# A selective scan on one core: two state products per GpSimd instruction, six fixed buffers for scanned states

## The chip, the cores and the metric

The kernel runs on one core of one Trainium2 chip. Its time is the device time of one execution in microseconds (us). Three executions took 8322.33, 8327.16 and 8331.08 us, so the median is 8327.16. The engines are TensorE (PE in the profile, its weight loads PEld), VectorE (DVE), ScalarE (ACT), GpSimd (POOL) and SyncE (SP), whose queue issues all DMAs. PE's clock has two levels, 1.2 and 2.4 GHz; the profile gives the granted clock as a share of the upper one.

## The reference, cut to what matters

The input is 1024 channels of 64 x 64 pixels. A first layer normalises and mixes along channels; its output, as 4096 tokens of 1024, goes through a bidirectional selective scan, which takes most of the time:

```python
def _direction(x_bdl, conv_w, conv_b, xproj_w, dtproj_w, dtproj_b, A_log, Dv):
    xc = conv(x_bdl) + conv_b                      # 4 taps, each of 2048 channels alone
    x_dbl = xc @ xproj_w.T                         # 64 for dt, 16 for B, 16 for C
    dt = x_dbl[..., :64] @ dtproj_w.T + dtproj_b
    Bm, Cm = x_dbl[..., 64:80], x_dbl[..., 80:]
    xc = jnp.clip(xc, -10.0, 10.0)                 # u
    delta = softplus(clip(dt, 1e-05, 1.0) + dtproj_b)
    # for each channel d and each of 16 states n, along the tokens:
    #   h = exp(delta * A[d, n]) * h + (delta * u) * B[n];  y = sum_n h * C[n]
    return y + xc * Dv

y = (y_fwd + y_bwd) * silu(z)
out = y @ out_proj_w.T
```

## The kernel before, in words

The stages run one after another: channel norm, pixel variance, a scan over channels, token norm, `stage_scan`, `stage_out`. The change is all in `stage_scan`, from about 700 to 7280 us.

In `stage_scan` the work is cut into 256 units, `b` in the code: first 128 of the backward direction, then 128 of the forward one. 16 units, one for each block of 128 channels, share a chunk of 512 tokens. A unit has 16 steps, one for each state `n`, and each engine has its own hand-written order within them (its function `unit`); semaphores tie the engines together. While unit b is scanned, the engines also prepare what comes later: delta of unit b + 1 (ACT), the input projection for x 17 units ahead or for z of this unit (PE, L836, copied by ACT at step 7, L1014), the convolution and projection of unit b + 17 (PE L843 and L848). The last 16 backward units have no input projection, the last 16 forward units no convolution.

For each state, ACT writes the decay exp(delta A) into one of two banks `da` (L1074), DVE scans (L1231), and ACT saves the last column (L1054, at the step two later). The scanned state is then multiplied by C and summed over the states in PSUM (`yT`) by transposing matmuls on PE. There are three ways for that:

- 10 states (`VN`) are scanned into PSUM (`h`, two slots), multiplied by DVE (L1241, which also waits for the save of that state) into one of six slots of `hc`, and transposed by PE (L962).
- 4 states (`PN` = 2, 5, 8, 11) are scanned into SBUF (`hs`), multiplied by GpSimd (`weigh_c`, L1188) into `hp`, and transposed by PE (L923) at steps `POOL_AT` = 5, 8, 11, 14.
- 2 states (`TN` = 4, 10) are scanned into `hs`, transposed by PE into `in_ps` at steps 8 and 12 (`turn`, L858), copied by ACT at steps 12 and 15 (L1040), and multiplied with the diagonals of C by PE (`add_turned`, L867). GpSimd makes the diagonals once a chunk (L1154).

`hs` has four slots which the six states of a unit use in turn, so the scan of a state waits until the one four places back has been read. GpSimd also clips xc to u (L1163), forms du = delta u (L1166), and multiplies du with B for four states at a time (`weigh_b`, L1179) into the ring `w` of four groups. Its order in unit b is: weights of group 2; product 2; weights of group 3; product 5; u and du of unit b + 1; product 8; in the first unit of a chunk two diagonals; weights 0 of unit b + 1; product 11; weights 1 of unit b + 1. At step 10 ACT multiplies u with D (`ud`, L1106), which PE adds at step 11 (L954). ACT copies the finished `yT` of unit b - 1 at step 2 of unit b (L1033), once PE has added its last product. SyncE loads xc after du, and at the end of a chunk the B and C rows of the next one (`broadcast`), each group when its last reader in the old chunk is done.

## Time and profile before

| | |
|---|---|
| median of three runs | 8327.16 us |
| profiled execution | 8327.64 us |
| its span, first to last instruction | 8325.9 us |
| busy PE / DVE / ACT / POOL, share of the span | 87% / 87% / 64% / 81% |
| mean granted clock of PE | 0.948 |
| weights with B on POOL, 128x2048 | 1023 of 4541 ns |
| scans on DVE, 128x512 | 2560 of 1280 ns into PSUM, 1536 of 1265 ns into SBUF |
| products with C on DVE / on POOL | 2560 of 678 ns / 1024 of 1276 ns |

How to read it: busy times are of one profiled execution. They are averages over stages, and in the scan stage DVE and POOL are both busy nearly all the time, so what sets the pace has to be read from the waits and from the timeline of a unit. In the timeline neighbours of one kind are merged (x2), and a bracket gives the idle time before a group and what ended it.

### The profile page before, as it was taken

The page shows a single profiled execution, that of the slowest core. Times are in us where ns is not written, and L with a number is a line of the kernel's source. Part 1 is how long each engine was busy: PE and PEld are TensorE (multiplying, and loading weights), DVE is VectorE, ACT ScalarE, POOL GpSimd, SP SyncE. Part 2 cuts the span into 40 slices and gives each one's busy share as a digit, 9 for nine tenths or more (in the row PEclk, how much of TensorE's full clock was granted, in tenths as well). Part 3 has the DMA queues.
Part 4 walks back from the last instruction along what each step waited for, and adds up shares of the span by engine and source line. Part 5 has one row for each costly group of instructions (what it writes and reads, how often), then busy time and mean ns, then how long its engine had stood idle before and what let it go on. Part 6 is the DMA issues. An engine that isn't in the chain of part 4 may idle for free. (4 is left out here: it accounts for less than half of the span.)

```text
span 8325.9 us, 116063 instructions
## 1 busy us (share of the span) xinstructions
PE 7232.1 (87%) x32656; PEld 4473.8 (54%) x32656; DVE 7202.0 (87%) x7790; ACT 5330.5 (64%) x12487; POOL 6737.9 (81%) x2833
## 2 busy tenths in 40 slices
PE   7568989998999899977899899899888987779999
PEld 3243555555555555555555555555555555534444
DVE  6921999999999999999999999999999999934444
ACT  3743777777777777776777777777777776610000
POOL 0612999999999999999999999999999999921110
PEclk9789999999999999988899999999999998889999
DMA  3273232313232323221323232323232322154342
GB/s 86 76 199 135 66 117 69 117 66 117 69 117 66 117 69 117 67 98 43 105 76 127 80 129 75 128 80 127 76 128 81 124 98 82 44 199 139 134 141 75
DMA packets 540822, 843.96 MB, mean 101 GB/s; under 512 B 112576, under 2 KB 260032, under 8 KB 522816
## 3 DMA queue, kind: packets, MB, share of 16 engines
q1 hardware_dynamic: 540224, 837.03, 30.5%
q8 instruction: 248, 4.06, 0.2%
q14 instruction: 350, 2.87, 0.1%
HBM read 583.83 MB, written 253.02 MB: 101 GB/s over the span
## 5 line engine op out<-in xcount | busy, mean ns | idle before, releaser
L1179 POOL TENSOR_TENSOR scan_w<-scan_du,scan_bcast_b 128x2048 f32<-128x2048 f32 x1023 | 4633.4, 4541 | 3.6 <-DMA scan_bcast_b<-bc 3.6
L1231 DVE TENSOR_TENSOR_SCAN scan_h<-scan_da,scan_state,scan_w 128x512 f32<-128x512 f32 x2560 | 3178.7, 1280 | 36.6 <-ACT scan_da L1074 21.3
L1074 ACT ACTIVATE scan_da<-scan_delta,scan_prm 128x512 f32<-128x512 f32 x4096 | 2804.3, 685 | 0.0
L962 PE MATMUL scan_yT<-all_ident,scan_hc 128*128 128x128 f32 x10240 | 1514.7, 279 | 768.1 <-DVE scan_hc L1241 767.5
L962 PEld LDWEIGHTS scan_yT<-all_ident,scan_hc 128*128 128x128 f32 x10240 | 1184.8, 142 | 1447.9 <-DVE scan_hc L1241 1068.5
L1231 DVE TENSOR_TENSOR_SCAN scan_hs<-scan_da,scan_state,scan_w 128x512 f32<-128x512 f32 x1536 | 1906.1, 1265 | 59.4 <-PE scan_in_ps L858 41.0
L836 PE MATMUL scan_in_ps<-scan_hn,scan_win 128*128 128x512 f32 x3840 | 1730.8, 593 | 13.5 <-issue 13.5
L1241 DVE TENSOR_TENSOR scan_hc<-scan_h,scan_bcast_c 128x512 f32<-128x512 f32 x2560 | 1652.5, 678 | 38.4 <-ACT scan_state L1054 36.7
L1188 POOL TENSOR_TENSOR scan_hp<-scan_hs,scan_bcast_c 128x512 f32<-128x512 f32 x1024 | 1306.5, 1276 | 60.0 <-issue 54.1
L836 PEld LDWEIGHTS scan_in_ps<-scan_hn,scan_win 128*128 128x128 f32 x3840 | 693.1, 191 | 714.7 <-issue 714.7
L1054 ACT ACTIVATE scan_state<-scan_h 128x1 f32<-128x1 f32 x2560 | 433.4, 169 | 868.6 <-DVE scan_h L1231 861.3
L843 PE MATMUL scan_dt_ps<-scan_x,scan_diag 128*128 128x512 f32 x1920 | 899.4, 612 | 1.1 <-ACT scan_x L1014 1.1
L1390 PE MATMUL out_o_ps<-out_yg,out_wout 128*128 128x512 f32 x2048 | 892.6, 595 | 0.0
L1358 POOL TENSOR_TENSOR out_yf<-out_yf,out_yb 128x512 f32<-128x512 f32 x128 | 162.9, 1273 | 740.5 <-DMA out_z<-z 740.5
L923 PE MATMUL scan_yT<-all_ident,scan_hp 128*128 128x128 f32 x4096 | 644.2, 282 | 2.8 <-POOL scan_hp L1188 2.5
L1390 PEld LDWEIGHTS out_o_ps<-out_yg,out_wout 128*128 128x128 f32 x2048 | 386.5, 191 | 465.8 <-issue 465.8
L1368 ACT ACTIVATE out_sz<-out_z 128x512 f32<-128x512 f32 x128 | 80.7, 630 | 822.2 <-DMA out_z<-z 822.2
L867 PE MATMUL scan_yT<-scan_h_turned,scan_c_diag 128*128 128x128 f32 x4096 | 594.4, 293 | 0.0
L843 PEld LDWEIGHTS scan_dt_ps<-scan_x,scan_diag 128*128 128x128 f32 x1920 | 355.9, 196 | 383.9 <-issue 383.9
L867 PEld LDWEIGHTS scan_yT<-scan_h_turned,scan_c_diag 128*128 128x128 f32 x4096 | 560.4, 212 | 0.0
L1040 ACT ACTIVATE scan_h_turned<-scan_in_ps 128x512 f32<-128x512 f32 x512 | 300.6, 587 | 338.4 <-PE scan_in_ps L858 338.4
L923 PEld LDWEIGHTS scan_yT<-all_ident,scan_hp 128*128 128x128 f32 x4096 | 499.2, 146 | 8.2 <-POOL scan_hp L1188 6.8
(128 smaller groups left out, 6761.9 us busy)
## 6 DMA issues: line engine op xcount, KB each, us to landing
yT<-scan_y_out SPq DMA_DIRECT2D x257, 256.0 KB, 2.0
scan_win<-winx SPq DMA_DIRECT2D x128, 512.0 KB, 3.6
xc<-scan_xc_out SPq DMA_DIRECT2D x256, 256.0 KB, 2.0
scan_xc<-xc SPq DMA_DIRECT2D x256, 256.0 KB, 3.9
scan_bcast_b<-bc SPq DMA_DIRECT2D x64, 1024.0 KB, 8.3
scan_bcast_c<-bc SPq DMA_DIRECT2D x64, 1024.0 KB, 7.7
scan_win<-winz SPq DMA_DIRECT2D x128, 512.0 KB, 4.7
scan_x<-x_pad SPq DMA_DIRECT2D x128, 257.5 KB, 2.6
```

The lines of the kernel that those rows point to most:

```text
L836: last = nc.tensor.matmul(bank, win[:, s, i], hn[:, i], start=(i == 0), stop=(i == KT - 1))
L843: last = nc.tensor.matmul(bank, diag[:, s, i], x[:, s, at:at + T], start=(i == 0), stop=(i == TAPS - 1))
L867: last = nc.tensor.matmul(yT[:, tb], c_diag[:, k, tb], h_turned[:, tb * P:(tb + 1) * P], start=False, stop=False)
L923: last = nc.tensor.matmul(yT[:, tb], hp[:, i, tb * P:(tb + 1) * P], ident[:], is_transpose=True, start=False, stop=False)
L962: last = nc.tensor.matmul(yT[:, tb], hc_slot(b, n)[:, tb * P:(tb + 1) * P], ident[:], is_transpose=True, start=(i == 0 and tb == 0), stop= ...
L1054: nc.scalar.activation(state_of(unit_, n_), h_slot(unit_, n_)[:, col:col + 1], ACT.Copy).then_inc(S["h_saved"], 1)
L1074: nc.scalar.activation(da[:, n % 2], delta[:, s], ACT.Exp, scale=decay(b, n)).then_inc(S["exp_done"], 1)
L1179: nc.gpsimd.tensor_tensor(w[:, g], du[:, s].unsqueeze(1).to_broadcast([P, G, T]), bcast_b[:, g * G:(g + 1) * G], ALU.mult).then_inc(S["w_d ...
L1188: nc.gpsimd.tensor_tensor(hp[:, i], h_slot(b, n), bcast_c[:, n], ALU.mult).then_inc(S["hp_done"], 1)
L1231: nc.vector.tensor_tensor_scan(flip(b, h_slot(b, n)), flip(b, da[:, n % 2]), flip(b, w[:, n // G, n % G]), state_of(b, n), ALU.mult, ALU.a ...
L1241: nc.vector.tensor_tensor(hc_slot(b, n), h_slot(b, n), bcast_c[:, n], ALU.mult).then_inc(S["hc_done"], 1)
L1390: last = nc.tensor.matmul(o_ps[:, q % 2], wout[:, q, b], yg[:, g, b], start=(b == 0), stop=(b == DB - 1))
```

## The change

GpSimd multiplies two states in one instruction of 128x2x512: states 2 and 5, then 8 and 11. The C rows of the two lie three rows apart in `bcast_c`, the scanned states side by side in `hs`, which now has six slots, one for each state of `PN` and `TN`. Each scan into `hs` waits for the reader of the same slot one unit earlier. GpSimd's order becomes: weights 2; products 2 and 5; weights 3; the diagonals if there are any; u and du of the next unit; weights 0; products 8 and 11; weights 1. PE adds the products of 2 and 5 at step 8 and those of 8 and 11 at step 14. u and du have one buffer each, so u waits for `ud` of the unit before; `ud` moves from step 10 to step 5 on ACT.

```diff
--- before.py
+++ after.py
@@ -31,7 +31,7 @@
 SN = sorted(PN + TN)
 VN = [n for n in range(NS) if n not in SN]
 NV, NP, NTN, NSN = len(VN), len(PN), len(TN), len(SN)
-NHS = 4
+HS = {n: i for i, n in enumerate(PN + TN)}
 NW = 4
 EPS_C, EPS_HW, EPS_T = 1e-6, 1e-5, 1e-5
 FMAX = 3.4028234663852886e38
@@ -567,12 +567,12 @@
         xc = sc.sb("xc", [P, 2, T])
         state = sc.sb("state", [P, 2 * DB * NS])
         v = sc.sb("v", [P, T])
-        delta, u, du = (sc.sb(n, [P, 2, T]) for n in ("delta", "u", "du"))
+        delta, u, du = sc.sb("delta", [P, 2, T]), sc.sb("u", [P, T]), sc.sb("du", [P, T])
         ud = sc.sb("ud", [P, T])
         w = sc.sb("w", [P, NW, G, T])
         hc = sc.sb("hc", [P, NOUT, T])
 
-        hs, hp = sc.sb("hs", [P, NHS, T]), sc.sb("hp", [P, NP, T])
+        hs, hp = sc.sb("hs", [P, NSN, T]), sc.sb("hp", [P, NP, T])
         c_diag, h_turned = sc.sb("c_diag", [P, NTN, TB, P]), sc.sb("h_turned", [P, T])
         y_out = sc.sb("y_out", [P, 2, TB, P])
 
@@ -618,7 +618,7 @@
 
         def h_slot(b, n):
             if n in SN:
-                return hs[:, (b * NSN + SN.index(n)) % NHS]
+                return hs[:, HS[n]]
             return h[:, (b * NV + VN.index(n)) % 2]
 
         def hc_slot(b, n):
@@ -651,7 +651,7 @@
                 return [(b, NORMAL)]
             return [(a, when) for a, when in inputs_of(b) if back(a)]
 
-        POOL_AT = [5, 8, 11, 14]
+        POOL_AT = [8, 8, 14, 14]
 
         def turn_steps(b):
             if b == 0:
@@ -916,8 +916,9 @@
             def unit(b):
                 ins = inputs_of(b)
                 for n in range(NS):
-                    if n in POOL_AT:
-                        i = POOL_AT.index(n)
+                    for i in range(NP):
+                        if n != POOL_AT[i]:
+                            continue
                         pe.wait_ge(S["hp_done"], b * NP + i + 1 + NP)
                         for tb in range(TB):
                             last = nc.tensor.matmul(yT[:, tb], hp[:, i, tb * P:(tb + 1) * P], ident[:],
@@ -1099,11 +1100,11 @@
                         ln_step(b + 1)
                     if nxt and n == (8 if late else 6):
                         delta_step(b + 1)
-                    if n == 10:
+                    if n == 5:
                         act.wait_ge(S["skip_loaded"], 2 * DB * LOAD)
                         act.wait_ge(S["u_done"], b + 1)
                         act.wait_ge(S["yT_copied"], b + 1)
-                        nc.scalar.activation(ud[:], u[:, s], ACT.Copy,
+                        nc.scalar.activation(ud[:], u[:], ACT.Copy,
                                              scale=skip[:, block_of(b):block_of(b) + 1]).then_inc(S["ud_done"], 1)
                     for a, when in ins:
                         if n == when["xc"]:
@@ -1159,49 +1160,48 @@
 
                 s = b % 2
                 pool.wait_ge(p_in[s], (b // 2 + 1) * (NPL * LOAD))
-                hold(pool, S["ud_done"], b + 1, S["passed"])
-                nc.gpsimd.tensor_scalar(u[:, s], xc[:, s], 10.0, -10.0, ALU.min, ALU.max).then_inc(S["u_done"], 1)
+                hold(pool, S["ud_done"], b + 2, S["passed"])
+                nc.gpsimd.tensor_scalar(u[:], xc[:, s], 10.0, -10.0, ALU.min, ALU.max).then_inc(S["u_done"], 1)
                 pool.wait_ge(S["u_done"], b + 1)
                 pool.wait_ge(S["delta_done"], b + 1)
-                nc.gpsimd.tensor_tensor(du[:, s], delta[:, s], u[:, s], ALU.mult).then_inc(S["du_done"], 1)
+                nc.gpsimd.tensor_tensor(du[:], delta[:, s], u[:], ALU.mult).then_inc(S["du_done"], 1)
 
             def weigh_b(b, g, single=False):
 
-                s = b % 2
                 pool.wait_ge(S["du_done"], b + 1)
                 pool.wait_ge(b_loaded[g], (b // DB + 1) * LOAD)
                 pool.wait_ge(S["scan_done"], b * NS + (g * G + G - NW * G + SCR))
                 if single:
                     for i in range(G):
-                        nc.gpsimd.tensor_tensor(w[:, g, i], du[:, s], bcast_b[:, g * G + i],
+                        nc.gpsimd.tensor_tensor(w[:, g, i], du[:], bcast_b[:, g * G + i],
                                                 ALU.mult).then_inc(S["w_done"], 1)
                 else:
-                    nc.gpsimd.tensor_tensor(w[:, g], du[:, s].unsqueeze(1).to_broadcast([P, G, T]),
+                    nc.gpsimd.tensor_tensor(w[:, g], du[:].unsqueeze(1).to_broadcast([P, G, T]),
                                             bcast_b[:, g * G:(g + 1) * G], ALU.mult).then_inc(S["w_done"], G)
 
             def weigh_c(b, i):
 
-                n = PN[i]
-                pool.wait_ge(c_loaded[n // G], (b // DB + 1) * LOAD)
-                pool.wait_ge(S["scan_done"], b * NS + (n + 1 + SCR))
-                pool.wait_ge(S["hp_used"], b * NP + i + 1)
-                nc.gpsimd.tensor_tensor(hp[:, i], h_slot(b, n), bcast_c[:, n], ALU.mult).then_inc(S["hp_done"], 1)
+                first, second = PN[i], PN[i + 1]
+                for n in (first, second):
+                    pool.wait_ge(c_loaded[n // G], (b // DB + 1) * LOAD)
+                pool.wait_ge(S["scan_done"], b * NS + (second + 1 + SCR))
+                pool.wait_ge(S["hp_used"], b * NP + i + 2)
+                nc.gpsimd.tensor_tensor(hp[:, i:i + 2], hs[:, HS[first]:HS[first] + 2],
+                                        bcast_c[:, first:second + 1:second - first], ALU.mult
+                                        ).then_inc(S["hp_done"], 2)
 
             def unit(b):
                 nxt = b + 1 < NU
                 weigh_b(b, 2)
                 weigh_c(b, 0)
                 weigh_b(b, 3)
-                weigh_c(b, 1)
-                if nxt:
-                    scan_input(b + 1)
-                weigh_c(b, 2)
                 if b % DB == 0:
                     for k in range(NTN):
                         make_diagonal(b, k)
                 if nxt:
+                    scan_input(b + 1)
                     weigh_b(b + 1, 0)
-                weigh_c(b, 3)
+                weigh_c(b, 2)
                 if nxt:
                     weigh_b(b + 1, 1)
 
@@ -1220,13 +1220,11 @@
                 dve.wait_ge(S["exp_done"], b * NS + n + 1 + NS + 1)
                 if n < G or n % G == 0:
                     dve.wait_ge(S["w_done"], b * NS + (n + 1 if n < G else n + G))
-                if n in SN:
-                    g = b * NSN + SN.index(n) - NHS
-                    if g >= 0 and SN[g % NSN] in PN:
-                        dve.wait_ge(S["hp_done"], g // NSN * NP + PN.index(SN[g % NSN]) + 1 + NP)
-                    elif g >= 0:
-                        dve.wait_ge(S["h_turn_mm"], g // NSN * NTN + TN.index(SN[g % NSN]) + 1)
-                else:
+                if n in PN:
+                    dve.wait_ge(S["hp_done"], b * NP + PN.index(n) + 1)
+                elif n in TN and b:
+                    dve.wait_ge(S["h_turn_mm"], (b - 1) * NTN + TN.index(n) + 1)
+                elif n in VN:
                     dve.wait_ge(S["hc_done"], b * NV + VN.index(n) + 1)
                 nc.vector.tensor_tensor_scan(flip(b, h_slot(b, n)), flip(b, da[:, n % 2]), flip(b, w[:, n // G, n % G]),
                                              state_of(b, n), ALU.mult, ALU.add).then_inc(S["scan_done"], 1)
```

## Rows read from the trace of the kernel before

**Rows 1.** groups by line and shape: busy us, mean ns, idle before

```profile
L1188 POOL TENSOR_TENSOR scan_hp<-scan_hs,scan_bcast_c 128x512 f32<-128x512 f32 x1024 | 1306.5, 1276 | 60.0 <-issue 54.1 <-DMA scan_bcast_c<-bc 3.4 <-DVE scan_hs L1231 1.9
...
L302 POOL TENSOR_TENSOR norm_xn<-norm_xn,norm_rstd 128x1024 f32 x28 | 65.4, 2355 | 0.0
...
L1154 POOL TENSOR_TENSOR scan_c_diag<-scan_bcast_c,all_ident 128x512 f32<-128x512 f32 x32 | 39.9, 1267 | 0.0
```

**Rows 2.** busy us (instructions) by stretch, then the granted clock of PE

```profile
1000.00:2000.00 1000.00, 904.59 (x4442) 580.09 (x4440) 989.10 (x1032) 768.26 (x1871) 988.15 (x403) 0.97 0.28 94
...
1422.60:1426.00 3.40, 3.40 (x12) 2.21 (x11) 3.40 (x5) 1.51 (x4) 3.40 (x3) 0.50 0.08 12
...
3620.00:4020.00 400.00, 287.93 (x1410) 201.22 (x1409) 369.07 (x384) 275.07 (x678) 366.91 (x151) 0.81 0.16 48
```

**Rows 3.** what DVE waited for from 780 to 7280 us: total, times, longest

```profile
DVE scan_hs L1231 <- PE scan_in_ps L858: 41.0, 66, 1.9
DVE scan_hc L1241 <- ACT scan_state L1054: 36.7, 105, 0.5
```

**Rows 4.** timeline of POOL over one unit: start, us, operation, count

```profile
1375.58 9.04 POOL L1179 TENSOR_TENSOR scan_w<-scan_du,scan_bcast_b 128x2048 f32<-128x2048 f32 x2
1384.58 1.26 POOL L1188 TENSOR_TENSOR scan_hp<-scan_hs,scan_bcast_c 128x512 f32<-128x512 f32 x1
1385.81 4.53 POOL L1179 TENSOR_TENSOR scan_w<-scan_du,scan_bcast_b 128x2048 f32<-128x2048 f32 x1
...
1391.66 0.61 POOL L1163 TENSOR_SCALAR scan_u<-scan_xc 128x512 f32<-128x512 f32 x1
...
1399.33 1.28 POOL L1188 TENSOR_TENSOR scan_hp<-scan_hs,scan_bcast_c 128x512 f32<-128x512 f32 x1
...
1416.64 0.61 POOL L1163 TENSOR_SCALAR scan_u<-scan_xc 128x512 f32<-128x512 f32 x1
```

**Rows 5.** timeline of DVE over two units, with idle time and releaser

```profile
1379.21 2.45 DVE L1231 TENSOR_TENSOR_SCAN scan_h<-scan_da,scan_state,scan_w 128x512 f32<-128x512 f32 x2
...
1385.12 2.43 DVE L1231 TENSOR_TENSOR_SCAN scan_hs<-scan_da,scan_state,scan_w 128x512 f32<-128x512 f32 x2
...
1404.00 2.46 DVE L1231 TENSOR_TENSOR_SCAN scan_h<-scan_da,scan_state,scan_w 128x512 f32<-128x512 f32 x2
...
1428.05 1.36 DVE L1241 TENSOR_TENSOR scan_hc<-scan_h,scan_bcast_c 128x512 f32<-128x512 f32 x2 [0.35 <-ACT scan_state L1054]
1429.32 2.46 DVE L1231 TENSOR_TENSOR_SCAN scan_h<-scan_da,scan_state,scan_w 128x512 f32<-128x512 f32 x2
```

**Rows 6.** timeline of PE's matmuls, end of one unit and middle of the next

```profile
1402.67 0.60 PE L923 MATMUL scan_yT<-all_ident,scan_hp 128*128 128x128 f32 x4
1403.54 0.66 PE L962 MATMUL scan_yT<-all_ident,scan_hc 128*128 128x128 f32 x4 [0.28 <-DVE scan_hc L1241]
...
1405.37 3.60 PE L836 MATMUL scan_in_ps<-scan_hn,scan_win 128*128 128x512 f32 x8
...
1421.83 0.66 PE L962 MATMUL scan_yT<-all_ident,scan_hc 128*128 128x128 f32 x4 [2.29 <-DVE scan_hc L1241]
```

**Rows 7.** timeline of ACT, second half of the same unit

```profile
1388.58 0.60 ACT L1014 ACTIVATE scan_x<-scan_in_ps 128x512 f32<-128x512 f32 x1
...
1389.44 0.69 ACT L1074 ACTIVATE scan_da<-scan_delta,scan_prm 128x512 f32<-128x512 f32 x1
...
1392.43 0.71 ACT L1106 ACTIVATE scan_ud<-scan_u,scan_skip 128x512 f32<-128x512 f32 x1
```

**Rows 8.** timeline of DVE in the slow stretch, scans of state 11

```profile
3860.05 1.28 DVE L1231 TENSOR_TENSOR_SCAN scan_hs<-scan_da,scan_state,scan_w 128x512 f32<-128x512 f32 x1 [1.88 <-PE scan_in_ps L858]
...
3887.35 1.28 DVE L1231 TENSOR_TENSOR_SCAN scan_hs<-scan_da,scan_state,scan_w 128x512 f32<-128x512 f32 x1 [1.88 <-PE scan_in_ps L858]
```

**Rows 9.** timeline of DVE at the ends of two chunks, scan of state 8

```profile
1592.77 1.28 DVE L1231 TENSOR_TENSOR_SCAN scan_hs<-scan_da,scan_state,scan_w 128x512 f32<-128x512 f32 x1 [1.21 <-ACT scan_da L1074]
...
1996.17 1.28 DVE L1231 TENSOR_TENSOR_SCAN scan_hs<-scan_da,scan_state,scan_w 128x512 f32<-128x512 f32 x1 [1.20 <-ACT scan_da L1074]
```

## The prediction, made before the changed kernel was run

> **What bounds the kernel now.** I read the profile in this order: costliest groups, busy time by stretch, what VectorE (DVE) waits for, then one unit engine by engine. A unit is one block of 128 channels over 512 tokens in one direction; the scan stage has 256, and times "in the unit" count from DVE's first scan. GpSimd (POOL) and DVE are both busy for about 99% of an ordinary stretch [rows 2], so busy shares can't say which one sets the pace. The unit does. POOL goes round in 24.98 us (from one u to the next), packed without a gap [rows 4]: four weight products at 4.50, four state products at 1.23, u and du about 2.1 together. DVE needs 24.79 us when nothing holds it (1379.21 to 1404.00) and took 25.32 in the next unit, where it waited 0.35 for ScalarE's (ACT) save of a state [rows 5]. POOL is ahead: it ends the product of state 11 at 1400.61, and TensorE (PE) takes it at 1402.67 [rows 4, 6]. So DVE with its small waits sets the end, and POOL is a few tenths behind it in rate. DVE waits 41.0 us for PE's turning of a state (L858) and 36.7 for the save [rows 3].
>
> Two places are worse. Between 3620 and 4020 us the units have no input projection for PE, its granted clock is 0.81 [rows 2], and the unit takes 27.30 us (3860.05 to 3887.35). In each of them the scan of state 11 waits 1.88 us for the turn of state 4, which has to leave one of the four slots of hs [rows 8]. This stretch holds some 28 of the 41 us. And each chunk of 16 units takes 403.4 us, 6.8 more than 16 x 24.79; at its end a scan waits 1.2 for ACT's decay [rows 9].
>
> **Part by part.**
>
> Two products in one instruction. A 128x1024 product on POOL took 2.355 us against two of 1.276 [rows 1]; with starts some 0.04 before the previous end it costs 2.31 instead of 2 x 1.23, 0.15 less, twice a unit: POOL's round falls to about 24.70. The bounds are 0 saved (the pair runs like two) and 0.4 (a pair saves all of what precedes the first element; not more, since 512 elements of the 128x2048 instruction alone are 4.5/4 = 1.13). POOL was not the bound, so this gains nothing by itself. A second input that jumps over two other states of bcast_c between its halves is in no row. The Trainium skill (GPSIMD Engine Reference, Performance pitfalls for Q7 kernels) says that a read whose step is above 8 bytes costs about half as much again per element; the steps here are 4 bytes but for the one jump, and no row shows such a jump. If it counted, it is the rival below.
>
> Six fixed slots. A scan into hs now waits for its own reader of one unit earlier, long done. The 41.0 us of waits for turns go. What is late next in the slow stretch: the convolution is still slowed by the clock, and ACT's copy of its result stands in front of the decay of state 11, some 0.2 (0 to 0.5) late. With 0.1 for other waits I take 25.1 per unit there instead of 27.30: 2.2 x 16 = 35 us.
>
> PE's order. The products of 2 and 8 move from steps 5 and 11 to 8 and 14: about 0.44 us of PE each (four transposes, 0.60 with the overlap [rows 6]). The turn of state 4 comes at most 0.44 later, which nobody but ACT's copy at step 12 now sees. The turn of state 10 comes 0.44 earlier (0.87 at half clock), and with it ACT's copy and the save behind it. I take the 0.35 waits for the save as gone; DVE's unit is then near 24.79 but for what follows.
>
> ud at step 5. ACT has room at step 10 (it waited for a scan there) and little between 5 and 8: the new 0.65 us pushes the decays of 6 and 7 back; decay 8 started at 1389.44, behind the wait for the scan of 6, and ended 0.3 before its scan [rows 7]. Going through ACT's queue with those durations, decay 7 ends 0.04 late and decay 8 about level: 0.08 per unit, bounds 0 and 0.3. Queued behind it are the copy of in_ps, every later decay, and so DVE.
>
> POOL's new order. The pair 2,5 needs scan 5, which ends 8.34 into the unit (1387.55) [rows 5]: start 8.45, end 10.8; weights of group 3 to 15.3; u and du to 17.3; weights of the next unit to 21.8; pair 8,11 from 21.8 to 24.2. POOL waits 0.15 at scan 5. Nothing is lost against DVE directly: each group of weights ends 2 to 3 us before its scan, where it was 4 to 6. u and du in one buffer: u waits for ud (done at about 8, wanted at 15.4), du follows its readers on POOL; nothing. SyncE's load of xc waits for du, which comes 3 us later than before but before SyncE gets there; nothing, and up to 1 us if not. Its loads of bcast_c for groups 2 and 3 wait for the last product of a chunk, 2.5 us later; the reader is the second diagonal at about 16 in the next unit, and I take nothing (0 to 1.5 per chunk).
>
> PE at step 14. PE took the product of 11 at 1402.67, 23.46 in the unit, and from the next group at 1403.54 to the input projection at 1405.37 it needs 1.83 [rows 6]. Now the pair comes at 24.2, and behind it on PE stand two product groups (0.87), the 1.83, and the whole input projection. That starts at 26.9 in place of 26.16: 0.65 after today's in the new unit. In today's kernel such a shift exists every third unit and costs the scan of state 8 about 0.08, by the copy of in_ps (1388.58) ahead of decay 8 [rows 7]. It overlaps the 0.08 of ud. Unit: 24.79 + 0.09 = 24.88.
>
> Start of a chunk. Two diagonals of 1.27 us [rows 1] once a chunk lie on POOL. They were covered by POOL's lead, now spent on waiting for scan 5. The pair 8,11 then ends at 26.6, PE stands still for nearly 4 us before it, and the copy of yT, the input projection and the scan of state 8 come 2.5 late. PE's clock has fallen behind shorter idle: after 2.29 us of waiting at 1421.83 it was 0.50 from 1422.60 to 1426.00, the lower of its two levels, 1.2 GHz [rows 2, 6], which costs half of 3.4. So 2.5 to 4.2 per chunk. The last unit of a chunk, with one dt matmul ahead of its projection, has its wait of 1.2 [rows 9], plus about 0.5: 1.76.
>
> Sum of an ordinary chunk: 396.6 + 16 x 0.09 + 1.76 + (2.5 to 4.2) = 402.3 to 404.0, middle 403.1, against 403.4: about 0.3 less, 15 times, 4 us. The slow chunk: 16 x 2.2 = 35 less, minus some 4 for its own ends, which the long unit covers now: 31. Together 35. The profiled execution took 8327.64 us with a span of 8325.9, 0.5 above the median of 8327.16. 8327.6 - 35 = 8292.6, say 8293.
>
> **Rivals.**
> 1. GpSimd is the bound, and its saving goes through. For it: 24.98 against 24.79 in rate. Against: its lead and its gapless round beside DVE's waits, and the new order ties it to scan 5. Then each round gives 0.26 x 256 = 67 and the slow stretch 33: 8228.
> 2. The slow stretch stays at about 27.3, because PE's clock and not the slot holds it (the turn's own lateness is PE's; the copy of the convolution takes its place). Ordinary chunks as above: 8324.
> 3. The pair saves nothing. POOL's round stays 24.96, above 24.88: 0.08 x 240 = 19 back, 8312.
> 4. Slower: PE's clock falls in the new wait at step 14. Before: the wait there was 0.28 (1403.54). Now about 1.3, from 22.9 to 24.2. If the clock falls behind it as behind 2.29, the stretch at half clock lies on the input projection, and the 1.7 us go through the copy of in_ps into the scan of 8. Once in three units, as falls come now: 85 x 1.7 = 145, 8438; only at more chunk ends and some units, 8345. It decides from a wait near 2 us; PE's other wait shrinks from 2.29 to about 1.8 as hp groups stand before it.
> 5. The jump in bcast_c costs half of a product's time for the pair, 1.1 us: POOL's round becomes 26.9, 2.0 x 240 = 480, 8775. By the skill's rule read widely; nothing in the rows speaks for it.
>
> **How the numbers follow.** Forecast 0.55, with 8270 to 8320 as its own range, of which 0.50 lies below 8310. Rival 1 0.12, rival 2 0.12, rival 3 0.08, rival 4 0.11, rival 5 0.02. Faster by over 0.2% (17 us; a measurement of this kernel tells no less from no change) 0.50 + 0.12 = 0.62; same 0.05 + 0.12 + 0.08 = 0.25; slower 0.13. Range: the ordinary unit is known to 0.1 (25 us over 256), the chunk starts to 1.5 x 16; the low end covers half of rival 1, the high end the mild form of rival 4: 8245 to 8345.
>
> **What would show it.** Right: pairs of 2.35 on POOL; no wait of a scan for L858; units of 24.9; the slow stretch near 25.1; POOL idle 0.1 to 0.2 before the pair 2,5; PE waiting about 1.3 for the second pair; small waits of scans 7 and 8 for ACT; 4 us at each chunk's start. Wrong if the first pair follows without a wait and units are 24.7 (rival 1), if the stretch from 3620 keeps 27 (2), if PE's clock is below today's 0.97 in an ordinary stretch (4), or if a pair is over 2.5 (3, 5).

## The result and the profile after

The changed kernel took 8390.97 us (median of 4 runs, 8387.92 to 8408.71), the kernel before 8325.49 us beside it. The ratio is 1.0082 with a 95% interval of 1.0065 to 1.0100: about 68 us slower (65 by the medians), where the prediction had 35 us faster (8293 against the 8327.6 that it counted from). The profiled execution took 8387.92 us with a span of 8386.1.

A unit's time is counted from VectorE's first scan in it to the first scan of the next unit. A chunk of 16 units now takes 408.8 to 413.4 us in the backward half (chunks 2 to 7) and about 407 in the forward half, where it took about 403.4 and 402. Chunk 8, the slow stretch of [rows 8], fell from 436.6 to 413.5.

First the groups of GpSimd, which answer [rows 1] (busy us, mean ns, idle before):

```profile
L1189 POOL TENSOR_TENSOR scan_hp<-scan_hs,scan_bcast_c 128x1024 f32<-128x1024 f32 x512 | 1207.5, 2358 | 152.7 <-DVE scan_hs L1229 150.8 <-issue 0.7
...
L1155 POOL TENSOR_TENSOR scan_c_diag<-scan_bcast_c,all_ident 128x512 f32<-128x512 f32 x32 | 40.1, 1278 | 0.0
```

A pair takes 2.358 us, as the 128x1024 product of [rows 1] did (2.355); the jump over two rows of bcast_c costs nothing that shows. Next the busy time by stretch, which answers [rows 2] (the granted clock stands third from the end):

```profile
1000.00:2000.00 1000.00, 880.32 (x4375) 566.42 (x4374) 974.87 (x1018) 751.76 (x1839) 966.72 (x317) 0.99 0.27 89
3620.00:4020.00 400.00, 283.64 (x1480) 192.10 (x1480) 387.00 (x404) 293.43 (x716) 383.23 (x126) 0.86 0.22 71
```

The clock is no lower than before, in the mean even higher (0.99 against 0.97), yet VectorE is busy for 974.87 of 1000 us instead of 989.10. What it and the others wait for, from 780 to 7280 us, which answers [rows 3]:

```profile
PE scan_yT L924 <- POOL scan_hp L1189: 246.6, 196, 3.8
...
POOL scan_hp L1189 <- DVE scan_hs L1229: 147.8, 168, 17.3
DVE scan_hs L1229 <- ACT scan_da L1075: 79.7, 142, 2.8
DVE scan_hc L1239 <- ACT scan_state L1055: 75.1, 36, 4.9
...
ACT scan_y_out L1034 <- PE scan_yT L963: 157.2, 155, 5.6
```

The scans' waits for PE's turn of a state (41.0 us) are gone, as forecast. In their place VectorE waits longer for ScalarE (ACT): 79.7 for decays (before 16.3), 75.1 for saves (before 36.7), up to 4.9 us at a time. The other lines lead there: PE waits 246.6 us for GpSimd's pairs (before 2.5 us in all for the single products), and ACT waits 157.2 us for PE at its copy of yT (before 2.5). GpSimd in turn now waits 147.8 us for VectorE's scans (before 1.9), nearly all of it ahead of the pair 2,5, which can't start before scan 5 has ended. So the loss runs from GpSimd through PE and ACT into VectorE, and no engine on it is busier than it was.

An ordinary unit shows where that begins. GpSimd's timeline, which answers [rows 4] (start, us, operation, count, idle before):

```profile
1473.30 0.61 POOL L1164 TENSOR_SCALAR scan_u<-scan_xc 128x512 f32<-128x512 f32 x1
1474.00 1.27 POOL L1167 TENSOR_TENSOR scan_du<-scan_delta,scan_u 128x512 f32<-128x512 f32 x1
1475.40 4.54 POOL L1179 TENSOR_TENSOR scan_w<-scan_du,scan_bcast_b 128x2048 f32<-128x2048 f32 x1
1479.90 2.35 POOL L1189 TENSOR_TENSOR scan_hp<-scan_hs,scan_bcast_c 128x1024 f32<-128x1024 f32 x1
```

Counted from the unit's first scan at 1457.75, the second pair runs from 22.15 to 24.50. What PE (matmuls), ACT and VectorE make of it, in this order, which answers [rows 5 to 7]:

```profile
1482.31 1.09 PE L924 MATMUL scan_yT<-all_ident,scan_hp 128*128 128x128 f32 x8 [1.27 <-POOL scan_hp L1189]
...
1485.27 0.60 ACT L1034 ACTIVATE scan_y_out<-scan_yT 128x512 f32<-128x512 f32 x1 [0.52 <-PE scan_yT L963]
...
1493.01 0.60 ACT L1015 ACTIVATE scan_x<-scan_in_ps 128x512 f32<-128x512 f32 x1 [0.34 <-PE scan_in_ps L836]
...
1493.56 0.70 ACT L1075 ACTIVATE scan_da<-scan_delta,scan_prm 128x512 f32<-128x512 f32 x1
...
1494.29 1.28 DVE L1229 TENSOR_TENSOR_SCAN scan_hs<-scan_da,scan_state,scan_w 128x512 f32<-128x512 f32 x1 [0.29 <-ACT scan_da L1075]
```

PE stands for 1.27 us, its input projection comes late, ACT's copy of that (at 1493.01) stands in front of the decay of state 8 (at 1493.56), and scan 8 waits 0.29. In the backward half most units alternate between 24.84 and about 25.28 us.

Now a unit of the same kind, 150 us earlier. First PE's matmuls behind the pair, then ACT, then VectorE, then PE's clock by stretch for this unit and for the one above:

```profile
1328.32 0.65 PE L963 MATMUL scan_yT<-all_ident,scan_hc 128*128 128x128 f32 x4
1330.27 1.78 PE L924 MATMUL scan_yT<-all_ident,scan_hp 128*128 128x128 f32 x8 [1.29 <-POOL scan_hp L1189]
1331.84 1.06 PE L963 MATMUL scan_yT<-all_ident,scan_hc 128*128 128x128 f32 x4
...
1334.87 0.60 ACT L1034 ACTIVATE scan_y_out<-scan_yT 128x512 f32<-128x512 f32 x1 [2.19 <-PE scan_yT L963]
...
1335.98 0.16 ACT L1055 ACTIVATE scan_state<-scan_h 128x1 f32<-128x1 f32 x1
...
1336.27 0.69 DVE L1239 TENSOR_TENSOR scan_hc<-scan_h,scan_bcast_c 128x512 f32<-128x512 f32 x1 [1.49 <-ACT scan_state L1055]
```

```profile
1482.31:1485.71 3.40, 3.40 (x26) 3.08 (x27) 3.40 (x4) 2.88 (x9) 3.40 (x1) 1.00 0.01 2
...
1330.27:1333.67 3.40, 3.40 (x17) 3.40 (x18) 3.40 (x4) 2.41 (x8) 3.40 (x1) 0.53 0.01 2
```

PE waited 1.29 us, as long as above, but here its clock fell: 0.53 for 3.4 us, nearly all of it at the lower level of 1.2 GHz, and the same 8 transposes took 1.78 instead of 1.09. ACT's copy of yT came 4.3 us into the unit (1334.87 after 1330.59). In the kernel's order for ACT the save of state 1 stands behind that copy (it ran at 1335.98), and VectorE's product of state 1 waits for this save. The unit took 26.9 us. There are 11 such units of about 27 us in the middle of chunks, 10 of them in the backward half.

The start of a chunk is the worst case of the same chain. GpSimd, PE, ACT and VectorE around the second unit, which begins at 1636.49:

```profile
1627.06 2.51 POOL L1155 TENSOR_TENSOR scan_c_diag<-scan_bcast_c,all_ident 128x512 f32<-128x512 f32 x2
...
1636.25 2.35 POOL L1189 TENSOR_TENSOR scan_hp<-scan_hs,scan_bcast_c 128x1024 f32<-128x1024 f32 x1
...
1638.66 1.97 PE L924 MATMUL scan_yT<-all_ident,scan_hp 128*128 128x128 f32 x8 [3.77 <-POOL scan_hp L1189]
...
1644.13 0.60 ACT L1034 ACTIVATE scan_y_out<-scan_yT 128x512 f32<-128x512 f32 x1 [5.55 <-PE scan_yT L963]
...
1645.53 0.69 DVE L1239 TENSOR_TENSOR scan_hc<-scan_h,scan_bcast_c 128x512 f32<-128x512 f32 x1 [4.84 <-ACT scan_state L1055]
```

```profile
1638.66:1642.10 3.44, 3.44 (x16) 3.44 (x17) 2.03 (x3) 0.00 (x0) 3.44 (x1) 0.50 0.00 0
```

The two diagonals push the pair, PE stands 3.77 us and then runs at half clock, and VectorE stands 4.84 us. The second unit takes 30.6 us. The last unit before this chunk takes 28.8 (in the backward half it is 26.4 to 28.8); its scan of state 8, with 1.21 of waiting in [rows 9], now reads

```profile
1598.06 1.28 DVE L1229 TENSOR_TENSOR_SCAN scan_hs<-scan_da,scan_state,scan_w 128x512 f32<-128x512 f32 x1 [2.85 <-ACT scan_da L1075]
```

(the last unit of the chunk that ends at 1611.7 us). So the chunk from there, the longest of the ordinary ones, has 413.4 us: 16 x 24.83 = 397.3, 5.8 in the second unit, 4.0 in the last, 4.4 in two units whose clock fell (26.90 and 27.17 us; the granted clock is 0.57 and 0.63 at their starts, behind waits of 1.28 and 1.55), and 2 in the small waits of the others.

### The profile page after: what moved, and what is told of

Same layout as the page of the kernel before. It is cut to its first block and busy times, and to the rows that moved or that the text cites. A ratio compares the mean times of both kernels' runs of the same rounds, so it can differ in the third digit from the quotient of the medians.

```text
span 8386.1 us, 115551 instructions
## 1 busy us (share of the span) xinstructions
PE 7205.9 (86%) x32656; PEld 4457.8 (53%) x32656; DVE 7194.2 (86%) x7790; ACT 5316.2 (63%) x12487; POOL 6684.0 (80%) x2321
## 5 line engine op out<-in xcount | busy, mean ns | idle before, releaser
L963 PEld LDWEIGHTS scan_yT<-all_ident,scan_hc 128*128 128x128 f32 x10240 | 1203.7, 144 | 1220.2 <-DVE scan_hc L1239 756.4
L1239 DVE TENSOR_TENSOR scan_hc<-scan_h,scan_bcast_c 128x512 f32<-128x512 f32 x2560 | 1640.6, 671 | 76.7 <-ACT scan_state L1055 75.1
L1189 POOL TENSOR_TENSOR scan_hp<-scan_hs,scan_bcast_c 128x1024 f32<-128x1024 f32 x512 | 1207.5, 2358 | 152.7 <-DVE scan_hs L1229 150.8
L924 PE MATMUL scan_yT<-all_ident,scan_hp 128*128 128x128 f32 x4096 | 569.2, 284 | 249.4 <-POOL scan_hp L1189 249.0
L924 PEld LDWEIGHTS scan_yT<-all_ident,scan_hp 128*128 128x128 f32 x4096 | 475.8, 146 | 298.7 <-POOL scan_hp L1189 298.7
L1417 DVE COPY out_o<-out_o_ps 128x512 f32<-128x512 f32 x64 | 44.2, 691 | 525.9 <-PE out_o_ps L1388 316.9
```

Of the source, the lines that this page charges most:

```text
L924: last = nc.tensor.matmul(yT[:, tb], hp[:, i, tb * P:(tb + 1) * P], ident[:], is_transpose=True, start=False, stop=False)
L963: last = nc.tensor.matmul(yT[:, tb], hc_slot(b, n)[:, tb * P:(tb + 1) * P], ident[:], is_transpose=True, start=(i == 0 and tb == 0), stop= ...
L1189: nc.gpsimd.tensor_tensor(hp[:, i:i + 2], hs[:, HS[first]:HS[first] + 2], bcast_c[:, first:second + 1:second - first], ALU.mult).then_inc( ...
L1239: nc.vector.tensor_tensor(hc_slot(b, n), h_slot(b, n), bcast_c[:, n], ALU.mult).then_inc(S["hc_done"], 1)
```

## The experiments

All ran in three rounds beside the kernel before (8325 to 8327 us); ratios are to it. Chunk and unit times come from VectorE's scans in each run's trace.

**e1_slots_alone.** The kernel before with the six fixed slots, and with the single du buffer that the larger hs needs for room; products, their places and ud as before.

```diff
-    return hs[:, (b * NSN + SN.index(n)) % NHS]
+    return hs[:, HS[n]]
-            delta, u, du = (sc.sb(n, [P, 2, T]) for n in ("delta", "u", "du"))
+            delta, u, du = sc.sb("delta", [P, 2, T]), sc.sb("u", [P, 2, T]), sc.sb("du", [P, T])
```

> The kernel before with six fixed slots of hs alone (du in one buffer to make room; GpSimd's single products, its order, PE's steps and ud as before). Theory A (the slots are right, the late second pair is what costs): the 41 us of waits for the turn of a state go, the slow stretch falls from 27.3 to about 25.5 per unit, 8280 to 8290. Rival (the slow stretch is held by PE's clock): 8320 or more.

Measured: 8289.97 us, ratio 0.9957 (0.9941 to 0.9974). The slots bring about 35 us. So a gain of the size that the prediction counted on is there, and the loss is in the rest of the change. It doesn't lie where it was expected, though. By the profiled executions the scan stage is 41.5 us shorter: 19 in the slow chunk (436.6 to 417.8), 12 in the other backward chunks and 10 in the forward ones. In the slow stretch a unit is 26.2 on average, not about 25.5, and this is why (VectorE's scan of state 11):

```profile
3843.34 1.28 DVE L1229 TENSOR_TENSOR_SCAN scan_hs<-scan_da,scan_state,scan_w 128x512 f32<-128x512 f32 x1 [1.91 <-ACT scan_da L1074]
```

The wait for the slot is gone and one for ACT's decay has come in its place: that decay stands behind ACT's copy of the convolution, which waited 2.63 us for PE.

**e2_singles_in_new_order.** The changed kernel, each pair replaced by two instructions in its place.

```diff
-                nc.gpsimd.tensor_tensor(hp[:, i:i + 2], hs[:, HS[first]:HS[first] + 2],
-                                        bcast_c[:, first:second + 1:second - first], ALU.mult
-                                        ).then_inc(S["hp_done"], 2)
...
+                for k in (i, i + 1):
+                    n = PN[k]
...
+                    nc.gpsimd.tensor_tensor(hp[:, k], h_slot(b, n), bcast_c[:, n], ALU.mult).then_inc(S["hp_done"], 1)
```

> The changed kernel with each pair taken apart into two single products in the same places of GpSimd's order, each waiting for its own state. Theory A: product 5 alone starts at the end of scan 5 and ends 1.1 us before the pair did, everything behind it on GpSimd comes 1.1 us earlier, and with it PE's step 14 (second products done at 23.5 in the unit, not 24.5), though GpSimd does 0.1 us more work per pair: 8330 to 8350. Rival (the order is what costs, pairs help): 8395 or more.

Measured: 8334.57 us, ratio 1.0012 (1.0002 to 1.0021). Two single products take more of GpSimd's time than a pair, and the kernel is 56 us faster with them. PE's wait for the products, then that of e1 beside it, and GpSimd's products of 2 and 5 in a chunk's first unit, which begins at 1615.45:

```profile
PE scan_yT L924 <- POOL scan_hp L1188: 157.4, 275, 1.6
...
PE scan_yT L923 <- POOL scan_hp L1188: 152.9, 311, 2.2
```

```profile
1620.82 1.26 POOL L1188 TENSOR_TENSOR scan_hp<-scan_hs,scan_bcast_c 128x512 f32<-128x512 f32 x1
1623.93 1.28 POOL L1188 TENSOR_TENSOR scan_hp<-scan_hs,scan_bcast_c 128x512 f32<-128x512 f32 x1 [1.84 <-issue]
```

Two things differ from the changed kernel. The first product of the late two is released half-way, so PE waits 157.4 us instead of 246.6, and never over 1.6 instead of 3.8. And product 2 doesn't wait for scan 5. (The view names nothing that ended the wait of 1.84.) Product 5 starts at 8.48 us into the unit, right behind scan 5, and ends at 9.8, where the pair ends at 10.96. All that follows in this unit comes so much earlier. (Later in a chunk GpSimd's lead is used up, and product 5 ends at 11.4.) The second unit of a chunk is then 27.6 on average in the backward half instead of 30.1, and no unit of 27 is left in mid-chunk. VectorE's wait for saves is 25.5 us instead of 75.1, which is most of the 56. How much of it each of the two things brings, no run tells apart. The total of PE's wait is no price by itself: e1 has nearly the same one and is 45 us faster, with the waits spread over several steps of the unit. Merging halves the number of hand-overs, delays the first one, and lets the work start only when the later of two inputs is there.

**e3_second_pair_early.** The changed kernel with one call moved: the pair 8,11 ahead of the next unit's first weights instead of behind them.

```diff
                 if nxt:
                     scan_input(b + 1)
-                    weigh_b(b + 1, 0)
                 weigh_c(b, 2)
                 if nxt:
+                    weigh_b(b + 1, 0)
                     weigh_b(b + 1, 1)
```

> The changed kernel with the pair of 8 and 11 ahead of the weights of group 0 of the next unit on GpSimd; all else as changed. Theory A: PE no longer waits at step 14, units go at 24.9, the units of 27 in mid-chunk vanish, and at the start of a chunk only the weights of group 0 come about 2 us late: 8260 to 8290. Rival (ud at ACT's step 5, or the diagonals, cost the time): 8370 or more.

Measured: 8287.9 us, ratio 0.9956 (0.9939 to 0.9973): 103 us less than the changed kernel, for the place of one instruction. PE takes the pair without a wait, ACT's copy of yT has none either, and VectorE's wait for saves is 1.4 us where it was 75.1; its wait for decays is 37.9 where it was 79.7. PE, then ACT, and the totals from 780 to 7280 us:

```profile
1423.74 1.04 PE L924 MATMUL scan_yT<-all_ident,scan_hp 128*128 128x128 f32 x8
...
1427.53 0.59 ACT L1034 ACTIVATE scan_y_out<-scan_yT 128x512 f32<-128x512 f32 x1
```

```profile
DVE scan_hs L1229 <- ACT scan_da L1075: 37.9, 59, 1.3
DVE scan_h L1229 <- POOL scan_w L1179: 26.2, 15, 2.0
...
DVE scan_hc L1239 <- ACT scan_state L1055: 1.4, 3, 0.7
```

Ordinary backward units are 24.84, backward chunks 400.7 to 401.2. The chain is shown: take the lateness of the second pair away and all of the loss goes. What is late next is GpSimd itself, once a chunk: 15 waits for weights, 26.2 us in all, which make a chunk's first unit 26.9.

**e4_ud_at_step_10.** The changed kernel with ud back at step 10 of ACT.

```diff
-                    if n == 5:
+                    if n == 10:
```

> The changed kernel with ud back at ACT's step 10. Theory A: the scans 7 and 8 lose their small waits for ACT's queue, but the copies behind PE stay late, so 0 to 10 us less: 8380 to 8391. Rival (ud in the narrow part of ACT's queue costs the time): 8320 to 8340.

Measured: 8403.27 us, ratio 1.0100 (1.0084 to 1.0117). The shortest units are 24.79 instead of 24.84, so the place of ud costs 0.05 where nothing else holds; but nothing is won in all, and the time lies above the 8380 to 8391 that were expected. The late pair sets the end here too: 13 mid-chunk units of about 27 against 11. The 12 us to the changed kernel are not clear of the noise, since the two intervals overlap.

**e6_no_diagonals.** The changed kernel with GpSimd's diagonals made in the first chunk alone. The later chunks' products for states 4 and 10 then use the first chunk's C: that part of the computation is changed.

```diff
-                if b % DB == 0:
+                if b == 0:
                     for k in range(NTN):
                         make_diagonal(b, k)
```

> The changed kernel making the diagonals of C in the first chunk only (later chunks use the first chunk's). Theory: their 2.5 us on GpSimd are what makes the second unit of a chunk long (30.4 backward, 27.7 forward against 24.84): 59 us less, 8325 to 8345. Rival (the long units at chunk starts come from the B and C loads or the dt matmul): 8380 or more.

Measured: 8334.9 us, ratio 1.0012 (1.0003 to 1.0022): 56 us less, 3.7 for each of the 15 later chunks, as expected. The second unit of a chunk falls from 30.1 to 25.3 us on average in the backward half and from 28.1 to 25.1 in the forward one; the last one keeps its 26.3 to 28.8 (backward).

**e5_pe_kept_busy and e9_filler_backward_half.** How much of the loss is the clock, and how much is plain lateness? Both keep PE at work in its wait for the second pair, with transposes into a bank that nobody reads then; e5 in all units, e9 (whose last condition is `if i == 2 and b < NU // 2`) in the 128 of the backward half.

```diff
+            def fill(b):
+                pe.wait_ge(S["h_turn_copied"], b * NTN + NTN)
+                for _ in range(12 + (22 if b % DB == 0 else 0) + (9 if b % DB == DB - 2 else 0)):
+                    nc.tensor.matmul(in_ps[:, 0:P], ident[:], ident[:], is_transpose=True, start=True, stop=True)
...
+                        if i == 2:
+                            fill(b)
```

> The changed kernel with filler transposes on PE (into in_ps, overwritten by the next input projection) ahead of the wait at step 14: 12 of 0.11 us in each unit, 34 in the first of a chunk, 21 where no dt matmul stands there. They end at about the time the pair of 8 and 11 is done. Theory B (the late pair alone costs 0.2 to 0.3 per unit and 2.5 per chunk start; the rest of the loss is PE's clock falling in that wait): no unit of 27 in mid-chunk, the second unit of a chunk 27 to 28 instead of 30.4 backward, 8330 to 8355. Rival (the clock has no part; any further PE work makes it worse): 8391 or more.

Measured: 8462.28 us, ratio 1.0161 (1.0144 to 1.0178). The expectation is missed by over 100 us, and only in one half. Backward it went as expected: chunks of 405 to 407 instead of 409 to 413, steady units of 25.07, none of 27. Forward, chunks grew from 407 to between 420 and 424. PE's matmuls and its clock there:

```profile
4973.88 0.66 PE L970 MATMUL scan_yT<-all_ident,scan_hc 128*128 128x128 f32 x4 [1.95 <-DVE scan_hc L1246]
...
4976.47 1.91 PE L867 MATMUL scan_yT<-scan_h_turned,scan_c_diag 128*128 128x128 f32 x8
...
4980.73 1.47 PE L919 MATMUL scan_in_ps<-all_ident 128*128 128x128 f32 x12
4982.04 1.04 PE L931 MATMUL scan_yT<-all_ident,scan_hp 128*128 128x128 f32 x8
```

```profile
4974.38:4978.30 3.92, 3.92 (x17) 3.03 (x16) 3.92 (x5) 1.51 (x4) 3.92 (x2) 0.56 0.33 83
```

There the clock falls behind PE's other wait, 1.95 us at the product of state 9, which the fillers don't cover. The matmuls behind it run late at 0.56, no wait for the pair is left, and twelve fillers (1.3 us, from 4980.73 to 4982.04) stand in front of a pair that GpSimd has finished at 4980.26: PE takes it 26.3 us into the unit instead of 24.6. So in that half the run measured the fillers' own cost. Hence e9:

> As e5 (the changed kernel with filler transposes on TensorE ahead of its wait for GpSimd's first pair), but only in the 128 units of the backward half; the forward half is the changed kernel's. Theory (the missed forecast of e5 came from the forward half alone, where the fillers stood in the way of matmuls that run late there; the backward half lost about 34 us of the changed kernel's time to TensorE's clock falling in its wait for the pair): backward chunks 405 to 407 as in e5, forward chunks 405 to 409 as in the changed kernel, time 8350 to 8360. Rival (the fillers shift the cost into the forward half, or the backward gain was a chance of one run): time within 10 us of the changed kernel's 8391, backward chunks 410 to 413.

Measured: 8362.57 us, ratio 1.0045 (1.0029 to 1.0062), 28 us less than the changed kernel by the medians, and 2.6 above the range expected. In the profiled executions the backward chunks have 37 us less and the forward ones, at 407 on average, are what they were. The gain lies in the second unit of a chunk (30.1 to 27.5 on average), in the last one (28.8 to 26.9 where it was longest) and in the units of 27, of which none is left; ordinary units keep their mean, 25.07 against (24.84 + 25.28) / 2 = 25.06. So if the fillers cost nothing of their own here, as that mean suggests, then of the 10.5 us that an ordinary backward chunk of the changed kernel (411.3) has over one of e3 (400.9), some 5.6 are the clock's falls in the new wait (411.3 to 405.7), and 4.9 the late hand-over itself. For the forward half the split stays open.

**e10_singles_second_pair_early.** e3 with single products in place of the pairs: what does merging bring where the place is right?

> As e3 (GpSimd's products of states 8 and 11 ahead of w0 of the next unit), but with four instructions of one state each, in the places of the two pairs: tells what the merging itself brings once the place is right. Theory (merging saves GpSimd some 0.39 us a unit, 4 x 1.276 against 2 x 2.358 from the rows, and GpSimd with VectorE sets the unit): units above 24.84, 25.0 to 25.1, time 8310 to 8345. Rival (merging gives nothing in this order, since the first of two single products lets TensorE begin earlier and the clock then stays): 8280 to 8295, units 24.8 as in e3.

Measured: 8287.65 us, ratio 0.9954 (0.9938 to 0.9971), e3's time to 0.3 us. The theory of this run, 8310 or more, is wrong by its own sum. Two single products back to back don't take 2 x 1.277, as this timeline of GpSimd shows (e10 first, then a pair of e3):

```profile
1422.10 2.50 POOL L1188 TENSOR_TENSOR scan_hp<-scan_hs,scan_bcast_c 128x512 f32<-128x512 f32 x2
```

```profile
1434.11 2.35 POOL L1189 TENSOR_TENSOR scan_hp<-scan_hs,scan_bcast_c 128x1024 f32<-128x1024 f32 x1
```

2.50 against 2.35: 0.15 each, as the prediction had it, and not the 0.2 that the expectation took. The pairs do show in the backward half. There GpSimd works all but without a gap in e10 and sets the unit, 24.98 and chunks of 402.1 against 24.84 and 400.9. Forward it is the other way round, 402.4 against 403.4, and the 1.0 lies in a chunk's first unit (25.8 against 26.9). GpSimd's first products in such a unit, e10 (begins at 5635.04), then e3 (5629.25):

```profile
5642.29 2.53 POOL L1188 TENSOR_TENSOR scan_hp<-scan_hs,scan_bcast_c 128x512 f32<-128x512 f32 x2
```

```profile
5637.85 2.36 POOL L1189 TENSOR_TENSOR scan_hp<-scan_hs,scan_bcast_c 128x1024 f32<-128x1024 f32 x1
```

The single products start 7.2 us into the unit, ahead of the end of scan 5; the pair starts at 8.6, behind it. GpSimd so gives up its lead, and the weights that VectorE waits for come 1.0 later (26.8 against 25.8). In all: nothing.

**e7_one_diagonal_early and e8_and_ud_at_10.** Can the once-a-chunk wait of e3 be had back? e7 is e3 with the first diagonal ahead of the first pair, e8 is e7 with ud at step 10.

```diff
                 weigh_b(b, 2)
+                if b % DB == 0:
+                    make_diagonal(b, 0)
                 weigh_c(b, 0)
                 weigh_b(b, 3)
                 if b % DB == 0:
-                    for k in range(NTN):
-                        make_diagonal(b, k)
+                    make_diagonal(b, 1)
```

> The kernel of e3 (second pair ahead of the weights of group 0) with the diagonal of state 4 moved ahead of the first pair in the first unit of a chunk, where GpSimd waits for scan 5 anyway. Theory: weights 0 come 1.25 us earlier there, 15 times, so 15 to 19 us less than e3: 8268 to 8275. Rival (its C row is not there in time, or the first pair is delayed as much): 8288.

> The kernel of e7 with ud back at ACT's step 10. Theory: the scans 7 and 8 lose waits of 0.05 per unit, 12 us less than e7, 8256 to 8263, unless u then waits for ud. Rival (as in the changed kernel, where step 10 was 12 us slower): 8280 or more.

Measured: 8283.86 (0.9946, 0.9930 to 0.9963) and 8279.61 (0.9942, 0.9926 to 0.9959), the fastest of all. Both fall short of what was expected. e7 still has 15 waits for the weights:

```profile
DVE scan_h L1230 <- POOL scan_w L1179: 23.5, 15, 1.9
```

23.5 us instead of 26.2. The idle time at scan 5 that was to hide the diagonal (2.9 us in the changed kernel, at 1620.26) isn't there in e3's order: in a chunk's first unit the weights end 8.5 us into the unit and the pair starts at 8.6. With the diagonal in between the pair starts at 9.7, and the next weights come only 0.1 earlier. So the two diagonals, 2.5 us of GpSimd's work, found no slack in either place. In e8 ordinary backward units are 24.78 instead of 24.84, the 0.05 that ud costs at step 5. Against e3 the steps are 4 us each, less than the intervals.

## Why the prediction was wrong

**What held.** The pair's duration and the free jump (rivals 3 and 5 fall). The six slots: 41 us of waits gone, and e1 alone gives 8290. The slow stretch, forecast at 25.1 a unit, has 25.6 and not 27.3 (rival 2 falls); half a microsecond of that term was missing. That e1 comes so near to the 8293 is in part luck: the prediction had 35 us less in the slow chunk from the slots, and they alone gave 19, since the decay of state 11 came up to 1.9 late and not 0.2 (0 to 0.5); 22 us came from the other chunks, where it had counted 4 for the whole change. ud at step 5: 0.08 forecast, 0.05 measured. GpSimd's new order, in the unit at 1457.75: first pair at 8.60 (8.45 forecast), second pair's end at 24.50 (24.2), PE's wait 1.27 (1.3), input projection at 27.26 (26.9). Rival 1 falls too: units aren't 24.7.

**What failed** is what that timeline was taken to cost, in three terms of the sum.

1. *PE at step 14.* The prediction followed the lateness along one route, input projection, copy of in_ps, decay 8, and made it 0.09 per unit. That route gives 0.29 to 0.44, in every second unit. The clock makes it dear: the same wait of 1.27 to 1.29 us is followed by 1.00 in one unit and 0.53 in another, and then the unit takes about 27. This is rival 4, set at 0.11 with the remark that it decides near 2 us of waiting; falls already come behind 1.28. They are not the rule there: of 42 waits of 1.2 to 1.6 us for the second pair in the backward half, 10 were followed by a fall. Its price of 1.7 a fall was about right (26.9 and 27.2 against 25.28); with 11 such units, and with falls at the starts and ends of chunks, the measured time lies between its two sizes. Its sign did not show it: the clock from 1000 to 2000 us is 0.99, above the 0.97 of before, because falls elsewhere became fewer (in the backward half up to 3660 us the trace has 49 in the kernel before and 23 now).
2. *Start of a chunk*, 2.5 to 4.2 forecast, is 5.8. The prediction saw PE stand still for nearly 4 us (3.77) and the clock fall, and named the copy of yT as late. It didn't see that this copy stands in ACT's queue at step 2, in front of the save and the decays of the next states. So lateness on PE, which nobody else waits for at that moment, becomes a stop of VectorE: 4.84 us.
3. *The last unit*, 1.76 forecast, is 4.0 where it is longest, by the same two routes one after the other.

The chunk of 413.4 is 16.8 over the prediction's floor of 16 x 24.79 = 396.6: 5.8 and 4.0 for its two ends, 4.4 for two units with a fall, 2.0 for small waits, and 0.6 for units of 24.83 instead of 24.79. The prediction's terms came to 6.5. The six ordinary backward chunks are on average 8 longer than the forecast 403.1, the slow one is 8 longer than forecast, the first 4 longer, and the seven ordinary forward ones 5.5 longer each than forecast: some 100 us in all, the distance between 8293 and 8391. e3 shows that all of it hangs on the place of the second pair: with it moved, the kernel lands at 8288, beside the 8293 forecast for the change as it stands. The prediction's end was right for another kernel.

**What the whole change is worth.** e1 (8290), e3 (8288) and e10 (8288) can't be told apart. So the measurable gain is that of the slots; merging brings 0.15 us of GpSimd's time per pair and, even in the right place, no time of the kernel in sum (e3 against e10); and merging in the place that the change gave it costs 56 of the 103 us that are lost (e2 against the changed kernel), the place itself, with single products, the other 47 (e2 against e10).

## What to carry to other kernels

Before moving a producer later, follow its consumer's result through every in-order queue behind it, and not along the most obvious route alone: the copy of yT blocked saves and decays that have nothing to do with it. Merging two instructions on an engine saves the little between them (here 0.15 us), starts only when the later input is there, and hands over the first result later by one operation (here 1.1 us); where the consumer has no slack, the hand-over is the larger of the two. A new wait on TensorE of even 1.3 us has to be priced with the clock's fall behind it, and with its cost at the few places where it is longest.

## What the runs showed of the hardware

Two waits of TensorE of nearly the same length (1.27 and 1.29 us), with the same matmul ahead of them, left the clock at 1.00 in one case and took it to 0.53 for 3.4 us in the other. In the changed kernel's backward half 10 of 42 waits of 1.2 to 1.6 us at this place were followed by a fall. What decides between them no run here has shown. Other waits of 1.95 and 3.77 us were followed by 0.56 and 0.50. Keeping TensorE at work in the wait, backward, took the falls away behind it (no mid-chunk unit of 27 us in e9, 10 in the changed kernel; the clock from 1000 to 2000 us is 1.00 against 0.99). Forward, in e5, they came behind another wait (0.56 behind 1.95 us).

A product on GpSimd whose second input jumps from one row of bcast_c to the third after it costs what one without a jump does: 2.358 us against 2.355. The Trainium skill (GPSIMD Engine Reference, Performance pitfalls for Q7 kernels) has reads with a step above 8 bytes cost about half as much again. Its advice there is about the inner step, which is 4 bytes here. The one jump in 1024 elements is an outer step, and the trace shows nothing of such a cost for it.
